# Three warm-up matmuls fewer, opening loads in another order, VectorE sums regrouped

## The reference

```
W = weights[condition]                                  # (64, 64, 64)
y = einsum('bct,bcd->bdt', x, W)                        # conditioned x, 4096 tokens of 1024
scores = y @ Wr.T                                       # (4096, 64)
gates = softmax(top_k(scores, 16)); G = scatter(gates)  # 16 of 64 experts a token
h = einsum('nd,krd->nkr', y, A)                         # 1024 -> 64 x 16
out = x + 2.0 * einsum('nkr,kdr->nd', h * G, B)         # 1024 -> 1024
```

## Time and profile before

| what | value |
|---|---|
| median of three runs | 717.7 us |
| profiled execution, its own time | 717.68 us |
| its span, first to last instruction | 715.9 us |
| TensorE matmul busy (PE) | 710.5 us, 99% |
| VectorE busy (DVE) | 480.6 us, 67% |
| ScalarE busy (ACT) | 262.4 us, 37% |
| GpSimd busy (POOL) | 8.0 us, 1% |
| chain that ended last | PE 96%, DVE 3% |

### The profile page before, as it was taken

One profiled execution on the slowest core, in us unless ns is written; L12 is line 12 of the kernel. 1 busy time (PEld: TensorE's weight loads), 2 busy tenths in 40 slices (PEclk: granted clock), 3 DMA queues, 4 the chain that ended last, 5 costly groups with the idle time before them and its releaser, 6 DMA issues.

```text
span 715.9 us, 9189 instructions
## 1 busy us (share of the span) xinstructions
PE 710.5 (99%) x3422; PEld 598.0 (84%) x3422; DVE 480.6 (67%) x957; ACT 262.4 (37%) x499; POOL 8.0 (1%) x10
## 2 busy tenths in 40 slices
PE   9999999999999999999999999999999999999998
PEld 8887888888888888888888888888888888888886
DVE  4799999996537696845442868774544297788552
ACT  5576763524325431123322642132232264223200
POOL 0003000000000000000000000000000000000000
PEclk9999999999999999999999999999999999999999
DMA  9967589846786757566667775755767687546653
GB/s 329 404 256 292 178 284 401 301 202 241 286 323 216 296 207 275 179 225 213 258 250 278 255 289 170 272 189 194 285 214 250 259 305 265 183 148 193 236 219 145
DMA packets 56670, 178.41 MB, mean 249 GB/s; under 512 B 9650, under 2 KB 10802, under 8 KB 56114
## 3 DMA queue, kind: packets, MB, share of 16 engines
q1 hardware_dynamic: 54642, 173.89, 67.1%
q10 hardware_dynamic: 1984, 3.93, 1.5%
HBM read 131.66 MB, written 46.14 MB: 248 GB/s over the span
## 4 chain that ended last, share of the span: by engine, by line
PE 96%; DVE 3%; issue 0%; ACT 0%; POOL 0%; POOLq 0%
PE Pb L266 43%; PE Pb L248 40%; PE Cb L228 7%; PE S L282 4%; PE T L530 1%; DVE Op L181 1%; DVE Q L364 1%; DVE Wt L199 1%; PE T L299 0%; PE T L354 0%; DVE R L364 0%; DVE Cq L364 0%; PE Cb L543 0%; DVE Xo L181 0%; PE T L543 0%
## 5 line engine op out<-in xcount | busy, mean ns | idle before, releaser
L248 PE MATMUL Pb<-Op,Wt 128*128 128x512 f32 x1008 | 238.3, 392 | 0.9 <-DVE Op L181 0.9
L248 PEld LDWEIGHTS Pb<-Op,Wt 128*128 128x128 f32 x1008 | 187.6, 188 | 39.6 <-DVE Op L181 1.3
L266 PE MATMUL Pb<-Wt,Op 128*128 128x512 f32 x912 | 212.1, 391 | 0.0
L266 PEld LDWEIGHTS Pb<-Wt,Op 128*128 128x128 f32 x912 | 170.0, 188 | 34.7 <-DVE Op L181 0.3
L364 DVE TENSOR_TENSOR Q<-Pb,Q 128x512 f32<-128x512 f32 x112 | 77.3, 690 | 90.9 <-PE Pb L266 90.8
L266 PE MATMUL Pb<-Wt,Ox 128*128 128x512 f32 x432 | 100.8, 391 | 0.0
L266 PEld LDWEIGHTS Pb<-Wt,Ox 128*128 128x128 f32 x432 | 80.5, 188 | 16.3
L234 ACT COPY R<-Cb 128x512 f32<-128x512 f32 x60 | 35.2, 589 | 159.2 <-PE Cb L228 159.2
L181 DVE TENSOR_TENSOR Op<-R,Op 128x512 fp32r<-128x512 f32 x98 | 66.2, 700 | 19.0 <-ACT Op L179 19.0
L364 DVE TENSOR_TENSOR Cq<-Pb,Cq 128x512 f32<-128x512 f32 x64 | 44.0, 687 | 49.6 <-ACT Cq L375 30.9
L248 PE MATMUL Pb<-Ox,Wt 128*128 128x512 f32 x288 | 66.3, 389 | 0.0
(11 more groups left out here) (85 smaller groups left out, 425.7 us busy)
## 6 DMA issues: line engine op xcount, KB each, us to landing
Wt<-Wd SPq DMA_DIRECT2D x168, 512.0 KB, 4.7
Wd<-Wt SPq DMA_DIRECT2D x56, 512.0 KB, 3.7
Q<-in_x SPq DMA_DIRECT2D x32, 512.0 KB, 5.0
xc<-in_x SPq DMA_DIRECT2D x24, 512.0 KB, 4.1
out<-Q SPq DMA_DIRECT2D x32, 256.0 KB, 2.6
out<-Q SPq DMA_DIRECT2D x16, 512.0 KB, 2.8
BR<-in_B SPq DMA_DIRECT2D x3, 1024.0 KB, 7.6
BR<-in_x SPq DMA_DIRECT2D x10, 256.0 KB, 11.3
```

What stands on the lines that cost most here:

```text
L248: t = pe.run(lambda e, c=c, o=o, a=a, z=z: e.matmul(Pb[:, b, :], Wt[:, k, a, 128 * c:128 * c + 128], part(o, z), start=fresh and (c, a, z) ...
L266: t = pe.run(lambda e, c=c, o=o, k=k, a=a, z=z: e.matmul(Pb[:, b, :], part(o, a)[:, 128 * i:128 * i + 128], Wt[:, k, z, :], start=fresh an ...
```

## The change

The number of warm-up matmuls goes from 15 to 12. Of the opening loads, x1(1,1) moves from ACT's queue to SP's, behind x1(0,1), and A(0,1) takes its place on ACT's queue; A(7) moves behind x0(4,0) and x0(5,0). A's sums are emitted as their loads arrive: S1 together with S3, S2 and S4 of the same tile, tiles 0 and 1 in step 1 of the first product, 2 and 3 in steps 2 and 3. T3 of B goes from GpSimd to VectorE, in two instructions of 128x1024, in the last two steps of the fourth product. The sums T1, T3 and T4 of y become one instruction of 128x2048 instead of four of 128x512 (T4 two of 128x1024 in slab 0). S2 of h is made one chunk ahead of its use: chunk 0 in the last step of Q2, the others in the steps of Q1.

```diff
-WARM = 15
+WARM = 12
...
-        for b in range(2):
-            load_x1(sp, 0, b)
-            load_x1(ac, 1, b)
+        load_x1(sp, 0, 0)
+        load_x1(ac, 1, 0)
+        load_x1(sp, 0, 1)
         load_an(ac, 0, 1)
+        load_x1(sp, 1, 1)
         ac.after(z_s)
         ac.run(lambda e: e.copy(nm[:, :], sS[:, 0:4]), False)
         load_an(sp, 1, 1)
...
         load_an(ac, 2, 0)
+        load_an(ac, 3, 0)
+        load_x0(sp, 4, 0)
+        load_x0(sp, 5, 0)
         load_an(sp, 7, 0, 2)
-        load_an(ac, 3, 0)
-        for i in range(4, 8):
-            load_x0(sp, i, 0)
+        load_x0(sp, 6, 0)
+        load_x0(sp, 7, 0)
...
-            def sum_t1(c):
-                t1[c] = add(ve, y11[c], y12[c], y11[c], split["y11"][c][1], R_ready[1][0], op=ALU.subtract)
+            def rows(k, lo, hi):
+                return R[:, k // 2, 4 * (k % 2) + lo:4 * (k % 2) + hi, :]
+
+            def sum_t1():
+                t1[:] = [add(ve, rows(0, 0, 4), rows(2, 0, 4), rows(0, 0, 4), *[split["y11"][c][1] for c in range(4)],
+                             R_ready[1][0], op=ALU.subtract)] * 4
...
             def sums_a(j):
                 A11, A12, A21, S1 = Q[:, j, 0:512], Q[:, j, 512:], Q[:, j + 4, 0:512], Cq[:, 2, j, :]
+                raw["S1", j] = add(ve, S1, A21, Q[:, j + 4, 512:], an_ready[4 + j][0])
...
                             a_unit(1, j, an_ready[j][0])
-                            for k in ((), (0, 1), (2,), (3,))[j]:
-                                raw["S1", k] = add(ve, Cq[:, 2, k, :], Q[:, k + 4, 0:512], Q[:, k + 4, 512:],
-                                                   an_ready[4 + k][0])
+                            if j == 1:
+                                sums_a(0)
+                                sums_a(1)
...
-                        if s == 0 and j == 3:
-                            sums_a(0)
+                        if s == 0 and j > 1:
+                            sums_a(j)
...
-                        if s == 0 and j == 3:
-                            for c in range(4):
-                                raw["T3b", c] = add(gp, BR[:, 1, c, :], BR[:, 2, c, :], BR[:, 1, c, :], B_ready[1],
-                                                    B_ready[2], op=ALU.subtract)
...
+                        if s == 0 and j > 1:
+                            lo, hi = 2 * j - 4, 2 * j - 2
+                            t = add(ve, BR[:, 1, lo:hi, :], BR[:, 2, lo:hi, :], BR[:, 1, lo:hi, :], B_ready[1],
+                                    B_ready[2], op=ALU.subtract)
+                            raw.update({("T3b", c): t for c in range(lo, hi)})
...
-                        raw["S2g", c] = add(ve, s2_place(c), q[0], q[3], Cq_ready[0][c], Cq_ready[3][c],
-                                            *((u_busy[c],) if s else (split["y22"][c][1], t2[c], t3[c])),
-                                            op=ALU.subtract)
+                        if c == 3:
+                            sum_s2(0)
...
                         if m == 1:
+                            if c < 3:
+                                sum_s2(c + 1)
```

More of the change, by code:

```diff
@@ L572, in adaln_ffn, with sum_t3, sum_t4 @@
             y11, y21, y12, y22 = [[R[:, k // 2, 4 * (k % 2) + c, :] for c in range(4)] for k in range(4)]
-            def sum_t1(c):
-                t1[c] = add(ve, y11[c], y12[c], y11[c], split["y11"][c][1], R_ready[1][0], op=ALU.subtract)
+            def rows(k, lo, hi):
[3 more added lines that the diff above has]
+                             R_ready[1][0], op=ALU.subtract)] * 4
             def sum_t2(c):
                 t2[c] = add(ve, y11[c], y22[c], y11[c], split["T1"][c][1], R_ready[1][1], op=ALU.subtract)
[L580 to L584, removed]
+            def sum_t3():
+                t3[:] = [add(ve, rows(2, 0, 4), rows(3, 0, 4), rows(2, 0, 4), *[split["y12"][c][1] for c in range(4)],
+                             R_ready[1][1], op=ALU.subtract)] * 4
+            def sum_t4(lo, hi):
+                t4[lo:hi] = [add(ve, rows(1, lo, hi), rows(1, lo, hi), rows(0, lo, hi),
+                                 *[split["y21"][c][1] for c in range(lo, hi)], *t2[lo:hi], R_ready[0][1],
+                                 op=ALU.subtract)] * (hi - lo)
             def sums_a(j):
                 A11, A12, A21, S1 = Q[:, j, 0:512], Q[:, j, 512:], Q[:, j + 4, 0:512], Cq[:, 2, j, :]
+                raw["S1", j] = add(ve, S1, A21, Q[:, j + 4, 512:], an_ready[4 + j][0])
                 raw["S3", j] = add(ve, A21, A11, A21, raw["S1", j], an_ready[j][0], op=ALU.subtract)
@@ L636, in adaln_ffn @@
                             a_unit(1, j, an_ready[j][0])
-                            for k in ((), (0, 1), (2,), (3,))[j]:
-                                raw["S1", k] = add(ve, Cq[:, 2, k, :], Q[:, k + 4, 0:512], Q[:, k + 4, 512:],
-                                                   an_ready[4 + k][0])
+                            if j == 1:
+                                sums_a(0)
+                                sums_a(1)
                         elif m == 1:
                             a_unit(2, j, raw["S1", j])
[L642 to L646, removed]
+                            Cq_busy[2][j] = (made[2, j], raw["S2", j])
                         elif m < 6:
@@ L657, in adaln_ffn @@
                             need("y11", c)
-                        if s == 0 and j == 3:
-                            sums_a(0)
+                        if s == 0 and j > 1:
+                            sums_a(j)
                         if s and j == 3:
-                            for c in range(4):
-                                sum_t1(c)
+                            sum_t1()
                     elif m == 1:
@@ L683, in adaln_ffn @@
                         if j == 1:
-                            for c in range(4):
-                                sum_t3(c)
+                            sum_t3()
                         if s == 0:
                             gated(1, j, 0)
+                        if s == 0 and j > 1:
[3 more added lines that the diff above has]
+                            raw.update({("T3b", c): t for c in range(lo, hi)})
                         if s and j == 3:
-                            for c in range(4):
-                                sum_t4(c)
+                            sum_t4(0, 4)
                     elif m == 4:
@@ L694, in adaln_ffn @@
                         if s == 0 and j > 1:
-                            sum_t4(2 * j - 4)
-                            sum_t4(2 * j - 3)
+                            sum_t4(2 * j - 4, 2 * j - 2)
                         if s:
@@ L738, in adaln_ffn, with sum_s2 @@
                         if (m, j) == (0, 3):
-                            for c in range(4):
-                                sum_t1(c)
+                            sum_t1()
             R_free[0] = split["T4"][3][1]
+            def sum_s2(c):
+                raw["S2g", c] = add(ve, s2_place(c), Cq[:, 0, c, :], Cq[:, 3, c, :], Cq_ready[0][c], Cq_ready[3][c],
+                                    *((u_busy[c],) if s else (split["y22"][c][1], t2[c], t3[c])), op=ALU.subtract)
             uses = ["G12", "G11", "S2", "S3", "G22", "S1", "S4"]
```

## The result

The changed kernel takes 719.59 us (median of nine, 718.95 to 719.75) against 717.69 for the kernel before on the same chip: ratio 1.0031, 95% interval 1.0022 to 1.0040. The ratio and its interval are estimated from the fast executions alone (one of the nine of the kernel before took 790.93 us), and so it is not exactly the quotient of the two medians, 1.0026. The changed kernel is slower, and 719.59 lies just above the upper end of the range, 719.2.

The account below looks back on a forecast made before the run. The prediction took TensorE's own work plus the holes in its timeline as the bound. 717.68 + 2.3 (front, the warm-up's 0.67 inside it) - 1.50 (holes) = 718.5 us, with the range 715.4 to 719.2.

Parts of the forecast that it names:

- Bound and holes: TensorE's whole timeline: its work plus holes set the time; holes of 1.29 and 0.21 us both go, minus 1.50.
- The reason given for the first hole: Before 63.12 us: GpSimd's T3 of B stretches two VectorE instructions by 2.1 us together, more than the hole.
- Loads: Front, P2's step 1: queues take turns by record, x0(1,0) lands at 17.0, step 1 starts near 17.9, plus 2.3 us.
- rival one: Opening loads: queues take turns by load, x0(1,0) lands at 15.1, plus 0.4 at the front, 716.6 us; chance 0.15.
- Warm-up: Front: six fewer passes bring everything behind the clock's rise 0.67 us earlier, not 1.28, used up in waiting for loads.
- the price of nothing for T3 on VectorE: Fourth product: T3's some 2.5 us covered by VectorE's earlier arrival; without cover, T2's operand late by at most 2.5 us.
- Rival three: Front: a DMA engine's lag reaches x0(1,0), landing at 18.4, step 1 at 19.3, plus 3.7, 719.9 us; chance 0.18.

Follow-up runs that it names:

- x1(1,1) in two: Changed kernel with x1(1,1) loaded as two loads of 128 KB on SP's queue instead of one of 256 KB: 719.95 us, one execution.
- T3 in the gaps: Changed kernel with B's two T3 instructions earlier on VectorE, at the third product's end and in the fourth's second step, where it waited: 718.57 us, ratio 1.0020.
- x1(1,1) on ACT: Changed kernel with T3 of B moved to where VectorE waited and x1(1,1) on ACT's queue behind A(0,1): 717.39 us, ratio 1.0006.
- both away: Changed kernel with T3 of B moved to where VectorE waited and the opening loads in the order of before: 716.51 us, ratio 0.9993.

## Why the prediction was wrong

**What every trace adds up to.** Two things account for each span: the start of step 1, and the holes behind it up to 128 us. "Sum" is both against the first trace of the kernel before, "span" the difference of the spans; they agree within 0.1 us.

| run | loads | T3 of B | step 1 | holes near 61, 109, 124 | sum | span |
|---|---|---|---|---|---|---|
| before | old | GpSimd | 15.62 | 1.17, 0, 0.11 | | |
| before once more | old | GpSimd | 15.53 | 1.21, 0, 0.09 | -0.1 | 0.0 |
| 12 warm-ups alone | old | GpSimd | 15.11 | 0.16, 0.23, 0.31 | -1.1 | -1.1 |
| new loads alone | new | GpSimd | 17.54 | 0.89, 0, 0.09 | +1.6 | +1.7 |
| changed kernel | new | VectorE, late | 17.53 | 0, 0.80, 0 | +1.4 | +1.4 |
| 15 warm-ups | new | VectorE, late | 17.04 | 0, 0.78, 0 | +0.9 | +0.9 |
| x1(1,1) in two | new | VectorE, late | 18.29 | 0, 0.80, 0 | +2.2 | +2.2 |
| S2 as before | new | VectorE, late | 17.69 | 0, 0.79, 0.32 | +1.9 | +1.9 |
| loads back | old | VectorE, late | 15.49 | 0, 0.78, 0 | -0.6 | -0.6 |
| T3 back | new | GpSimd | 17.21 | 0, 0, 0 | +0.3 | +0.3 |
| T3 in the gaps | new | VectorE, gaps | 17.59 | 0, 0, 0 | +0.7 | +0.7 |
| x1(1,1) on ACT | new, one moved | VectorE, gaps | 16.50 | 0, 0, 0 | -0.4 | -0.4 |
| both away | old | VectorE, gaps | 15.19 | 0, 0, 0 | -1.7 | -1.7 |
| A(0,1) in halves | old, one halved | VectorE, gaps | 15.55 | 0, 0, 0 | -1.3 | -1.3 |

**Bound and holes: right, but worth 1.28 us and not 1.50.** TensorE's row of work set the time, and the two old holes went. Their size was read against 2.72 us for a dense step, where these two steps take 2.84 and 2.82. The reason given for the first hole is not needed in full: with T3 back on GpSimd it is closed as well.

**Loads: the right mechanism, 0.4 us too much.** x1(1,1) was expected near 10.0 and came near 9.9, step 0 at 11.4 (11.28), x0(0,0) at 15.4 and x0(1,0) at 17.0, where the waits ended at 14.98 and 16.64. Step 1 started at 17.53 instead of 17.9: +1.91 for the +2.3 of the sum. By the ratios the new loads alone cost 2.3 us in the kernel before, and putting them back gives 1.9 in the changed one. Where both queues have records of 2 KB and more they kept step again: from 13.5 to 17 us, 307 and 308 records of 0.56 and 0.82 MB.

```profile
q10 hardware_dynamic: 308, 0.82, 61.4%
q1 hardware_dynamic: 307, 0.56, 42.9%
```

With the x1 loads' records of 1 KB they need not keep step: in the run with x1(1,1) in two, ACT's queue has 105 and SP's 69 from 4.3 to 4.75 us, all below 2 KB. The prediction's count of turns used one turn for each record there too, and the rate of 352 GB/s for x1(1,1) left out the dip. So that x1(1,1) came near 10.0 is partly luck.

The Trainium skill's rule that an engine drains a packet of several descriptors before it switches (DMA: Bandwidth & Descriptors, Queues, rings and completion order), read as one turn for a load, gave rival one 15.1 for x0(1,0); the trace has 16.6 and sides with turns by record. With x1(1,1) in two it was 17.4, so boundaries may cost something; that stays open.

**Warm-up: 0.67 was swallowed, as said, but its worth elsewhere was mis-sized.** With the old loads it meets the wait for A(0,1): step 0 starts 0.17 to 0.50 us earlier than 11.07 in four runs. When the clock rises is not fixed either. The 24 passes of the warm-up took 4.49 us in one execution and 5.49 in another (same count, at the two levels in other shares); the Trainium skill, TensorE: Matmul & The Clock Gate, What's actually happening, says that the point moves from run to run, and the traces agree.

**The step that failed is the price of nothing for T3 on VectorE.** I wrote that VectorE comes to the fourth product earlier by more than the 2.5 us that it then pays. It was early, but an engine that works in order cannot keep a lead: it waits for the next drain or cast, 1.02 and 1.40 us at 62 and 71 us. T3 stood behind the last of these waits, at the head of 57 us without any, and its 2.44 us came out at the first operand with less slack than that: the last piece of G12, in Q2. I had named T2's operand at the fifth product instead, and had not looked at the slack in Q2. In the kernel before, the remainder that the tenth matmul of Q2 needs was done at 110.18 and wanted at 108.52 + 9 x 0.227 = 110.56, 0.4 us of slack:

```profile
108.52 5.60 PE L266 MATMUL Pb<-Wt,Op 128*128 128x512 f32 x24
```

```profile
109.49 0.69 DVE L181 TENSOR_TENSOR Op<-Cq,Op 128x512 fp32r<-128x512 f32 x1
```

In the changed kernel it is done at 111.89 and was wanted at 109.24 + 2.04 = 111.28:

```profile
111.19 0.70 DVE L181 TENSOR_TENSOR Op<-Cq,Op 128x512 fp32r<-128x512 f32 x1
```

All five traces with T3 late on VectorE have this hole, 0.78 to 0.80 us, with either order of loads, and none of the five with T3 back on GpSimd or in the gaps has it. The ratios agree: without T3 on VectorE, or with it in the gaps, the ratio is 0.0011 below that of the changed kernel, and with the old loads it is 0.0011 below that of the loads put back: 0.8 us each time. Each of these differences alone is within its noise; what settles it is that the hole is there or not in ten traces.

**The sum with the measured terms** is 717.68 + 1.91 - 1.28 + 0.80 = 719.11, beside 719.13 in the profiled execution. The forecast was 718.5: the front was put 0.4 too high and the gain from the holes 0.2 too high, which offset each other in part, and 0.8 was missing. The other 0.46 up to the median of 719.59 lies in executions that no trace shows, and is open; without it the time would have been inside the range. Of the same size is the spread of the start of step 1, 17.04 to 17.69 with one order of loads. And in every experiment with a ratio the time differs from that of the kernel before by 0.2 to 1.2 us more, to the slow side, than the two traces do, which again says that both traces of the kernel before are of executions above its median. Rival three (719.9) had the right side but the wrong mechanism: x0(1,0) came at 16.6, not at 18.4.

## What to carry to other kernels

The two queues fed the same DMA engines and, with rows of 2 KB and more, shared them record by record (307 to 308), so a load moved from one queue to the other delayed everything behind it, x0(1,0) from 13.2 to 16.6 us. That a load with short rows costs more follows from the count of turns; no run tries it with other rows. Count turns and bytes up to the load that is wanted first, and not the place of a load in its own queue. Work added to an engine that runs in order is free in front of one of its waits; behind the last wait of a saturated stretch it can come out at the first operand with little slack, however early the engine was before (here 0.80 of 2.44 us did). Closing a hole or removing warm-up only uncovers the next wait: look which load or operand is wanted 0.2 us later before pricing it. And measure a hole against the same step without one, not against another step: 2.72 for 2.84 us made the gain 0.2 us too large.

## What was not expected of the hardware

Between 6 and 8 us the queues' rate dips in every trace, to 203 to 288 GB/s in its lowest microsecond, about where the turn of A(0,1) comes; the microseconds beside it move 300 and more in most. With that load halved over both queues the dip is there too (235), and the load did not land earlier. And GpSimd's additions stretch VectorE's two-operand ones from 0.68 to 1.78 us, yet leave a remainder that reads from PSUM (`Wt<-Cb`) at 0.68 in the same 6 us: what the work on GpSimd costs depends on which instructions it meets.
